# A post-norm decoder layer on one core: the last two down steps interleaved by token tile, transposed x2 in two buffers, side work one step earlier

## What is computed

```python
x = layernorm(x + attention(x))                    # 16 heads, causal, rotary
q, k = ctx @ Wq.T + bq, ctx @ Wk.T + bk            # cross attention, 256 -> 128
x = layernorm(x + einsum('bln,bmn->blm', x, softmax(q @ k.T)))
x = layernorm(x + (silu(x @ w_gate.T) * (x @ w_up.T)) @ w_down.T)   # hidden 2048
```

## Time and profile before

| | us |
|---|---|
| median of three runs | 1038.43 |
| the three runs | 1037.93 to 1039.27 |
| the profiled execution, device time | 1038.01 |
| its span in the trace | 1036.2 |
| TensorE busy | 974.7 |
| mean granted clock of TensorE | 0.99 of full speed |

### The profile page before, as it was taken

The page is one execution under the profiler, slowest core; times in us unless marked ns, Lnnn a source line. Parts: engine busy times, 40 slices in busy tenths (PEclk is TensorE's granted clock), DMA queues, the critical chain, the costliest instruction groups (busy, mean ns, idle before and its releaser), DMA issues.

```text
span 1036.2 us, 15732 instructions
## 1 busy us (share of the span) xinstructions
PE 974.7 (94%) x5416; PEld 789.4 (76%) x5416; DVE 628.6 (61%) x1344; ACT 492.7 (48%) x1075; POOL 352.3 (34%) x353
## 2 busy tenths in 40 slices
PE   7778999999998888999999999999999999999995
PEld 5557777777776666788888788888788888788883
DVE  5687778878775787545544565544665454653443
ACT  5576667767765684244432334432334332333330
POOL 2566646755755442322112132112041111121112
PEclk9999999999999999899999999999999999999998
DMA  5976576755864670262221252221252221243301
GB/s 219 243 190 180 158 182 155 224 146 148 239 159 115 178 209 1 92 237 88 92 92 61 91 208 88 92 92 62 92 218 97 78 86 61 92 173 97 115 2 41
DMA packets 45055, 134.53 MB, mean 130 GB/s; under 512 B 5425, under 2 KB 5553, under 8 KB 42161
## 3 DMA queue, kind: packets, MB, share of 16 engines
q1 hardware_dynamic: 44976, 133.52, 42.5%
HBM read 104.14 MB, written 25.17 MB: 125 GB/s over the span
## 4 chain that ended last, share of the span: by engine, by line
PE 77%; DVE 6%; POOL 5%; issue 5%; ACT 4%; DMA 2%; SPq 0%; POOLq 0%; DVEq 0%; ACTq 0%
PE pg L559 17%; PE pu L559 17%; PE pd L559 17%; PE pj L507 9%; PE pj L559 5%; PE pv L550 4%; PE ps L522 2%; ACT prob L714 2%; PE pa L535 2%; PE pb L535 2%; PE pj L565 1%; DVE prob L911 1%; POOL raw L1139 1%; POOL raw L1144 1%; DMA qk_scratch<-raw 1%
## 5 line engine op out<-in xcount | busy, mean ns | idle before, releaser
L1228 POOL TENSOR_TENSOR g_lo<-gated,g_hi 128x512 fp32r<-128x512 f32 x64 | 82.6, 1290 | 439.5 <-ACT g_hi L805 439.5
L714 ACT ACTIVATE prob<-prob,nmax 128x512 f32<-128x512 f32 (+3 forms) x256 | 143.7, 562 | 106.7 <-DVE nmax L911 106.3
L911 DVE CUSTOM_DVE_ANT_0 prob<-ps,mask 128x512 f32<-128x512 f32 (+3 forms) x256 | 122.9, 485 | 76.9 <-PE ps L522 73.5
L1017 DVE TENSOR_TENSOR dn_lo<-f_raw,dn_hi 128x512 fp32r<-128x512 f32 x64 | 51.3, 802 | 120.9 <-ACT dn_hi L789 120.9
L522 PE MATMUL ps<-ks,qs 128*128 128x256 f32 (+2 forms) x256 | 105.4, 413 | 12.8 <-DVE nmax L911 9.9
L1038 DVE SCALAR_TENSOR_TENSOR half<-th,pg 128x512 f32<-128x512 f32 x64 | 44.0, 688 | 104.3 <-ACT th L796 104.3
L559 PE MATMUL pd<-dn_hi,g_hi 128*128 128x512 f32 x256 | 101.0, 395 | 0.2 <-POOL g_lo L1228 0.2
L796 ACT ACTIVATE th<-pg 128x512 f32<-128x512 f32 x64 | 38.3, 598 | 131.7 <-PE pg L559 131.7
L559 PE MATMUL pd<-dn_lo,g_hi 128*128 128x512 f32 x256 | 99.7, 389 | 0.0
L559 PE MATMUL pd<-dn_hi,g_lo 128*128 128x512 f32 x256 | 99.7, 389 | 0.0
L805 ACT CAST g_hi<-gated 128x512 fp32r<-128x512 f32 x64 | 39.7, 621 | 120.4 <-DVE gated L1045 120.4
(11 more groups left out here) (177 smaller groups left out, 2215.8 us busy)
## 6 DMA issues: line engine op xcount, KB each, us to landing
f_raw<-in_w_ffn SPq DMA_DIRECT2D x64, 768.0 KB, 4.4
qs<-qk_scratch SPq DMA_DIRECT2D x64, 256.0 KB, 4.6
ks<-qk_scratch SPq DMA_DIRECT2D x60, 256.0 KB, 7.7
qk_scratch<-qk_hi SPq DMA_DIRECT2D x32, 256.0 KB, 2.0
qk_scratch<-raw SPq DMA_DIRECT2D x32, 256.0 KB, 2.1
res<-in_x SPq DMA_DIRECT2D x4, 1024.0 KB, 5.0
x_scratch<-res SPq DMA_DIRECT2D x4, 1024.0 KB, 5.2
x<-x_scratch SPq DMA_DIRECT2D x4, 1024.0 KB, 4.8
```

The lines of the kernel that those rows point to most:

```text
L714: act.activation(prob[:, t % PROBS, 0:w], prob[:, t % PROBS, 0:w], ACT.Exp, bias=nmax[:, n % 2, i:i + 1], scale=-1.0, accum_out=rsum[:, n ...
L911: dve.tensor_tensor_reduce(prob[:, t % PROBS, 0:w], ps[:, t % 2, 0:w], mask[:, S - w:S], -D ** -0.5, 3e38, ALU.add, ALU.min, accum_out=nma ...
L1017: dve.tensor_tensor(dn_lo[:, i % 2, :], f_raw[i % NR][:, 2 * KT * P:], dn_hi[:, i % 2, :].bitcast(F32), ALU.subtract).then_inc(dnlo_done, 1)
L1228: pool.tensor_tensor(g_lo[:, i % 2, :], gated[:], g_hi[:, i % 2, :].bitcast(F32), ALU.subtract).then_inc(glo_done, 1)
```

## The change

1. `x2T_hi` and `x2T_lo` get a second buffer; sequence `b` uses number `b % 2`.
2. The side work of `BESIDE` moves one step earlier, and the four `u` transposes are split: tiles 0 and 1 at j = 14, tiles 2 and 3 at j = 15. The load of the context of the sequence after next is issued one place earlier by SyncE, ahead of the store of the output and not behind it.
3. The last step (63) gets banks and buffers of its own: gate and up go to the two banks of `pj`, its halves to `last_hi` and `last_lo`. Its hidden products come before `down(61)`. ScalarE and VectorE split its gate and up weights at the end of step 61 instead of in step 62.
4. The down steps 62 and 63 are interleaved by token tile: three matmuls of step 62 and three of step 63 for tile 0, then tile 1, and so on. Each tile signals `tile_full`, and `finished` waits tile by tile.
5. The last layer norm of tiles 0, 1 and 2 is written by ScalarE, for which GpSimd makes a third small value `nmr2`; tile 3 stays on VectorE. Each tile is stored in a DMA of its own, 256 KB.

```diff
-BESIDE = {3: [("ctx", 0)], 4: [("c", 0)], 5: [("e", 0), ("e", 1)], 6: [("e", 2), ("e", 3)],
+BESIDE = {2: [("ctx", 0)], 3: [("c", 0)], 4: [("e", 0), ("e", 1)], 5: [("e", 2), ("e", 3)],
...
-          11: [("m", 0)], 12: [("m", 1)], 13: [("m", 2)], 14: [("m", 3)], 15: [("u", 0), ("u", 1), ("u", 2), ("u", 3)]}
+          10: [("m", 0)], 11: [("m", 1)], 12: [("m", 2)], 13: [("m", 3)], 14: [("u", 0), ("u", 1)], 15: [("u", 2), ("u", 3)]}
...
+    x2T_hi, x2T_lo = [x2T_hi0, x2T_hi1], [x2T_lo0, x2T_lo1]
...
+    def gate_bank(i):
+        return pj[:, 0, :] if i == STEPS - 1 else pg[:]
+    def up_bank(i):
+        return pj[:, 1, :] if i == STEPS - 1 else pu[:]
+    def gated_halves(i):
+        return (last_hi[:, 0, :], last_lo[:, 0, :]) if i == STEPS - 1 else (g_hi[:, i % 2, :], g_lo[:, i % 2, :])
+    def down_halves(i):
+        return (last_hi[:, 1, :], last_lo[:, 1, :]) if i == STEPS - 1 else (dn_hi[:, i % 2, :], dn_lo[:, i % 2, :])
...
@@ sync
-            if not last:
-                context(b + 1)
+            if b == 0:
+                context(1)
...
             reload(range(HT * b + 2, HT * b + (HT + 2 if not last else HT - NR)))
-            sp.wait_ge(ln_done[1], ST * (b + 1))
-            sp.dma_start(out[b * P:(b + 1) * P, :], fin[:]).then_inc(out_done, 16)
-        sp.wait_ge(out_done, 16 * B)
+            if b < B - 2:
+                context(b + 2)
+            if not last:
+                sp.wait_ge(ln_done[1], ST * (b + 1))
+                sp.dma_start(out[b * P:(b + 1) * P, :], fin[:]).then_inc(out_done, 16)
+        for s in range(ST):
+            if s < ST - 1:
+                sp.wait_ge(tile_done, s + 1)
+            else:
+                sp.wait_ge(ln_done[1], ST * (B - 1) + 1)
+            sp.dma_start(out[(B - 1) * P:B * P, s * E:(s + 1) * E], fin[:, s, :]).then_inc(out_done, 16)
...
@@ tensor
+        def last_down(i, s):
+            if s == 0:
+                pe.wait_ge(dnlo_done, i + 1)
+                pe.wait_ge(glo_done, i + 1)
+            cols = slice(s * P, (s + 1) * P)
+            return three(pd[:, s, :], 1, lambda k: [g[:, cols] for g in gated_halves(i)],
+                         lambda k: down_halves(i), False, i == STEPS - 1)
-        for i in range(1, STEPS):
+        for i in range(1, STEPS - 2):
...
-        down(STEPS - 1)
+        for i in (STEPS - 2, STEPS - 1):
+            hidden(i, 0)
+            hidden(i, 1)
+        down(STEPS - 3)
+        for s in range(ST):
+            last_down(STEPS - 2, s)
+            last_down(STEPS - 1, s).then_inc(tile_full, 1)
...
@@ scalar, at the end
+        for s in range(ST - 1):
+            act.wait_ge(nmr2_done, s + 1)
+            act.activation(fin[:, s, :], fin[:, s, :], ACT.Identity, bias=nmr2[:, s:s + 1],
+                           scale=rstd2[1][:, s, :]).then_inc(tile_done, 1)
...
@@ scalar and vector, in step(i)
-            if i < STEPS - 1:
+            if i < STEPS - 2:
                 gu_half(i + 1)
...
+            if i == STEPS - 3:
+                gu_half(i + 2)
...
@@ vector
+            if b == B - 1:
+                dve.wait_ge(tile_full, s + 1)
+            elif s == 0:
                 dve.wait_ge(d_full, HT * (b + 1))
...
-        for s in range(ST):
-            normalized(B - 1, 1, fin, s)
+        normalized(B - 1, 1, fin, ST - 1)
...
@@ gpsimd, at the end
         for s in range(ST):
             root(B - 1, 1, s)
+            if s < ST - 1:
+                pool.wait_ge(rstd2_done[1], ST * (B - 1) + s + 1)
+                pool.tensor_scalar(nmr2[:, s:s + 1], mv2[1][:, s, 0:1], rstd2[1][:, s, :], -1.0, ALU.mult, ALU.mult).then_inc(nmr2_done, 1)
```

More of the change, by code:

```diff
@@ L161, in program @@
     cqk_hi, cqk_lo = sb("cqk_hi", [P, 2, S], F32R), sb("cqk_lo", [P, 2, S], F32R)
-    x2T_hi, x2T_lo = sb("x2T_hi", [P, KT, S], F32R), sb("x2T_lo", [P, KT, S], F32R)
+    x2T_hi0, x2T_lo0 = sb("x2T_hi0", [P, KT, S], F32R), sb("x2T_lo0", [P, KT, S], F32R)
     f_raw = [sb(f"f_raw{n}", [P, 2 * KT * P + E]) for n in range(2)]
@@ L170, in program @@
     fin = sb("fin", [P, ST, E])
-    sb("unused", [P, 10884 - 1024 + 1024])
+    x2T_hi1, x2T_lo1 = sb("x2T_hi1", [P, KT, S], F32R), sb("x2T_lo1", [P, KT, S], F32R)
+    last_hi, last_lo, nmr2 = sb("last_hi", [P, 2, S], F32R), sb("last_lo", [P, 2, S], F32R), sb("nmr2", [P, ST])
+    sb("unused", [P, 4736])
+    x2T_hi, x2T_lo = [x2T_hi0, x2T_hi1], [x2T_lo0, x2T_lo1]
     flat = pT[:].rearrange("p h n -> p (h n)")
@@ L624, in hidden @@
                     pe.wait_ge(max_done, SCORES)
-                else:
+                elif i < STEPS - 1:
                     pe.wait_ge(gate_read, i)
-            elif i:
+            elif 0 < i < STEPS - 1:
                 pe.wait_ge(gated_done, i)
-            three((pg, pu)[u][:], KT, lambda k: (gu_hi[:, i % 2, u, k, :], gu_lo[:, i % 2, u, k, :]),
-                  lambda k: (x2T_hi[:, k, :], x2T_lo[:, k, :])).then_inc((g_full, u_full)[u], 1)
+            three((gate_bank, up_bank)[u](i), KT, lambda k: (gu_hi[:, i % 2, u, k, :], gu_lo[:, i % 2, u, k, :]),
+                  lambda k: (x2T_hi[i // HT % 2][:, k, :], x2T_lo[i // HT % 2][:, k, :])).then_inc((g_full, u_full)[u], 1)
         def down(i):
@@ L758, in t_half @@
             later, done, hi = {"t": (t1_full, t1hi_done, x1T_hi), "a": (a_full, ahi_done, att_hi),
-                               "u": (t2_full, t2hi_done, x2T_hi)}[kind]
+                               "u": (t2_full, t2hi_done, x2T_hi[b % 2])}[kind]
             filled(act, b, later, kind, n)
@@ L786, in dn_half @@
                 act.wait_ge(av_done, GROUPS)
-            if i >= 2:
+            if 2 <= i < STEPS - 1:
                 act.wait_ge(d_full, i - 1)
-            act.copy(dn_hi[:, i % 2, :], f_raw[i % NR][:, 2 * KT * P:]).then_inc(dnhi_done, 1)
+            act.copy(down_halves(i)[0], f_raw[i % NR][:, 2 * KT * P:]).then_inc(dnhi_done, 1)
         def step(i):
@@ L795, in step @@
                 act.wait_ge(gate_read, i)
-            act.activation(th[:], pg[:], ACT.Tanh, scale=0.5).then_inc(th_done, 1)
-            if i < STEPS - 1:
+            act.activation(th[:], gate_bank(i), ACT.Tanh, scale=0.5).then_inc(th_done, 1)
+            if i < STEPS - 2:
                 gu_half(i + 1)
             if j == HT - 1 and b < B - 1:
-                for s in range(ST):
-                    t_half(b + 1, "u", s)
+                for kind, n in BESIDE[j]:
+                    t_half(b + 1, kind, n)
             act.wait_ge(gated_done, i + 1)
-            if i >= 2:
+            if 2 <= i < STEPS - 1:
                 act.wait_ge(d_full, i - 1)
-            act.copy(g_hi[:, i % 2, :], gated[:]).then_inc(ghi_done, 1)
+            act.copy(gated_halves(i)[0], gated[:]).then_inc(ghi_done, 1)
             if b < B - 1:
@@ L976, in t_half @@
             hi_done, done, hi, lo = {"t": (t1hi_done, t1lo_done, x1T_hi, x1T_lo), "a": (ahi_done, alo_done, att_hi, att_lo),
-                                     "u": (t2hi_done, t2lo_done, x2T_hi, x2T_lo)}[kind]
+                                     "u": (t2hi_done, t2lo_done, x2T_hi[b % 2], x2T_lo[b % 2])}[kind]
             cols = slice(n * P, (n + 1) * P)
@@ L1044, in step @@
                 dve.wait_ge(glo_done, i)
-            dve.scalar_tensor_tensor(gated[:], half[:], 0.5, pu[:], ALU.mult, ALU.mult).then_inc(gated_done, 1)
+            dve.scalar_tensor_tensor(gated[:], half[:], 0.5, up_bank(i), ALU.mult, ALU.mult).then_inc(gated_done, 1)
             steps = BESIDE.get(j, []) if b < B - 1 else []
             if j == HT - 1 and b < B - 1:
-                for s in range(ST):
-                    t_half(b + 1, "u", s)
+                for kind, n in steps:
+                    t_half(b + 1, kind, n)
             beside(b + 1, steps)
@@ L1225, in step @@
             pool.wait_ge(ghi_done, i + 1)
-            if i >= 2:
+            if 2 <= i < STEPS - 1:
                 pool.wait_ge(d_full, i - 1)
-            pool.tensor_tensor(g_lo[:, i % 2, :], gated[:], g_hi[:, i % 2, :].bitcast(F32), ALU.subtract).then_inc(glo_done, 1)
+            hi, lo = gated_halves(i)
+            pool.tensor_tensor(lo, gated[:], hi.bitcast(F32), ALU.subtract).then_inc(glo_done, 1)
             if b < B - 1:
```

20 lines of the change are left out of this document (12 added, 8 removed).

## The result

| | before | changed |
|---|---|---|
| median, us | 1038.85 (4 runs, 1037.93 to 1040.30) | 1028.02 (4 runs, 1026.07 to 1029.37) |
| ratio of the changed kernel's time | | 0.9884, 95% interval 0.9869 to 0.9899 |
| profiled execution, device time | 1038.01 | 1029.37 |
| its span | 1036.2 | 1027.6 |

The changed kernel is 1.2% faster, 10.8 us by the medians; 1027.4 was forecast. Six more runs on another occasion gave 1028.88 us and a ratio of 0.9895 (0.9879 to 0.9911). Spans are given to 0.1 us, and differences that end at a span's end are no better than that.

What follows compares the result with a forecast made beforehand. TensorE, busy 94%, bounds the kernel; gains come only where it stands still or behind its last matmul. Terms 4.20 + 0.46 + 4.09 + 0.42 + 1.90 = 11.07 us off 1038.01 give 1026.9, as median 1027.4; range 1025.8 to 1031.0.

Steps and rivals of the forecast that it cites:

- Term 1: Three sequence ends: splitting the transposes over two steps removes TensorE's wait, 1.40 us each, 4.20 us in all.
- Term 2: Gap ahead of the last down step: down(61) and other matmuls cover the wait for the new halves, 0.46 us gained.
- The margin: Between last hidden product and first product needing the new halves: 3.40 us of matmuls cover 2.85 us, leaving 0.55.
- Term 3: Program end: interleaved down steps let VectorE's 6.20 us block of sums and moments start 4.09 us before TensorE's end.
- Term 4: Last tile's norm: GpSimd's two small operations run fast without VectorE's norms beside them, 0.42 us gained.
- Term 5: Final store: last 256 KB lands in 2.0 us where 1 MB took 3.9, 1.90 us gained.
- Side work: Moved one step earlier at no cost; second sequence's context, the tightest place, lands 2 us before ScalarE asks for it.
- A: Rival at the tail: four stores share one queue, GpSimd's pair stays slow, 1.90 + 0.42 us less gain, 1029.7; chance 0.07.
- B: Rival at the sequence ends: they keep their wait through another late partner, 1031.6 us; chance 0.04.
- C: Rival in sequences 1 and 3: TensorE reads the second x2T buffer slower; 1042.8 us at 20 ns per matmul; chance 0.03.
- D: Rival for the whole kernel: nothing measurable, sequence-end and VectorE gains both failing, 1036 us or more; chance 0.02.

Runs made afterwards that it cites:

- e4: Changed kernel with two x2T buffers, but all four x2 transposes together at j = 15; median 1032.98 us, ratio 0.9938 to the kernel before.
- e1: The changed kernel run again with no edit; median 1028.88 us, ratio 0.9895 to the kernel before.
- e3: Kernel before with only the changed sequence ends: two x2T buffers, side work one step earlier, context load ahead of the store; median 1035.22 us, ratio 0.9959.
- e6: Changed kernel with all four last norms on VectorE, still stored tile by tile; median 1030.51 us, ratio 0.9911 to the kernel before.
- e5: Changed kernel with one 1 MB store for the last sequence; median 1030.17 us, ratio 0.9913 to the kernel before.
- e7: Changed kernel with the last two down steps one after the other, not interleaved; median 1031.73 us, ratio 0.9928 to the kernel before.
- e8: Changed kernel with down(61) ahead of the hidden products of step 63; median 1031.80 us, ratio 0.9923 to the kernel before.
- e2: Changed kernel with the old sequence ends (one x2T buffer, side work in its old steps), so tail only; median 1031.97 us, ratio 0.9931.

## Why the prediction was right, term by term

Times of the changed kernel are those of its first profile.

| term | forecast, us | measured, us | how |
|---|---|---|---|
| 1, sequence ends | 4.20 | 4.05 | 3 x (5.90 + 2.72 - 3.64 - 3.63) |
| 2, gap ahead of the last down step | 0.46 | 0.45 | see below |
| 3, VectorE beside the down steps | 4.09 | 4.08 | last matmul's end to last `mv`: 6.30 before, 2.22 now |
| 4, GpSimd's pair | 0.42 | 0.44 | last `mv` to last norm: 1.41 before, 0.97 now |
| 5, store | 1.90 | 1.62 | last norm's end to the span's end: 4.27 before, 2.65 now |
| sum | 11.07 | 10.64 | |

**Term 1** has the right mechanism, shown by e4. A little is missing since the down step behind transposes took 2.76 to 2.77 us in this profile and 2.73 to 2.74 in the earlier trace rows. In e1's profile it is 2.73, and the two steps last 7.22 us, a gain of exactly the forecast 1.40 for each end. The same 0.03 us stands behind each of the other twelve pairs of transposes, 0.4 us, which makes up for the difference between the sum of 10.64 and the measured 10.2 of the second part. The profiles of e3 and e6 have the 2.77 too, those of e1, e5, e7 and e8 the 2.73 to 2.74, and in e2 and e4 both kinds stand in one execution; with 18 such steps it makes 0.5 us, nearly all of the 0.6 by which the changed kernel's two profiles differ. So it changes from one execution to another, with the same code; its cause stays open.

**Term 2.** From the gate product of step 62 to the end of the last matmul 84 matmuls are done in both kernels. The chain has that product at

```profile
1004.17 2.72 PE pg L559 x12
```

before and now at

```profile
1002.16 2.72 PE pg L588 x12
```

so it took 19.50 us before (to 1023.67) and 19.05 now (to 1021.21), which is 84 x 0.227: nothing stands still any more. The margin was forecast with 0.55 us. GpSimd ended `last_lo` at 1015.78 (1014.50 + 1.28):

```profile
1014.50 1.28 POOL L1284 TENSOR_TENSOR last_lo<-gated,last_hi 128x512 fp32r<-128x512 f32 x1 [4.15 <-ACT last_hi L849]
...
1016.06 0.19 PEld L588 LDWEIGHTS pd<-last_hi 128*128 128x128 f32 x1
1016.28 0.39 PE L588 MATMUL pd<-last_hi 128*128 128x512 f32 x1
```

The weight load of the first matmul behind the wait started at 1016.06 and the matmul at 1016.28. So 0.28 to 0.50 us were left, somewhat less than forecast, but enough. e8 shows what the order is worth when this cover is gone.

**Term 3.** VectorE runs through from 1017.23 to 1023.43, 6.20 us, the same as before; it is the slower of the two, as forecast. The interleaving and the signals by tile share the gain in halves (e7).

**Term 4.** The size was right, and e6 shows the cause. What the prediction said of the third small operation holds too: GpSimd needs 1.22 us a tile (1020.47 to 1021.69). ScalarE's norm of tile 2 ended 0.64 us behind the last `mv`, as it said (0.65).

**Term 5** is the term whose size was most off, by 0.28 us: 2.2 us to landing where the row of equal size gave 2.0. The row was of stores to the scratch, whose destination is one block of 2 KB rows; here the rows lie 8 KB apart in the output. Whether this or something else makes the 0.2 us wasn't tried; the last 0.1 is rounding. The last store took 2.2 in each of the kernels that store by tile with VectorE's pace.

**Side work.** ScalarE asked for the second sequence's context at 453.66, directly behind `g_hi` of step 2, and found it landed, as forecast; no wait for it stands in the trace.

**The rivals.** A needs stores in close order, and e6 has shown that the effect exists, with 0.7 us and not the 1.9 that A gave it, and why it stays away here. B is excluded by the chain at the sequence ends, C by the two `pg` pieces of 2.72 us that read different x2T buffers, and D by the runs.

**The medians.** The sum of the terms (10.6) and the medians' difference (10.8 and, beside e1, 10.5) agree; a single profiled pair (8.6) would have misled by 2 us. The forecast of 1027.4 was 0.6 us too low. Of this 0.4 lies in its starting point, the median of three runs (1038.43), which is 1038.85 with the fourth, and 0.2 in the terms (11.07 against 10.83 by the medians).

## What to carry to other kernels

Where two buffers take turns and tile n + 2 waits for tile n, put other work in between: half of the tiles a step earlier took away 1.4 us each time. It took a second buffer for what the tiles are written to; whether more `pj` banks would have done as well wasn't tried. At the end of a program, let the last accumulations run tile by tile, put work that needs nothing new between the last product and the first use of its result, and count for each engine behind it what it needs per tile; the slowest (here VectorE, 1.52 us against TensorE's 1.36) sets what is left. Store the last tile alone, but not in close order with the others.

## What the runs showed of the hardware

**The same code ahead of the change took between 437.0 and 441.8 us, and most of the difference is granted clock.** The attention part and step 0 aren't touched by any kernel here, so the same ScalarE operation can be looked up in each trace. The 121st starts between 84.7 and 86.2 us. From there to the 151st, 30 operations on, the table of stretches (start and end, length; PE, PEld, DVE, ACT and POOL busy; granted clock; DMA share; GB/s) has for the kernel before, e8, the changed kernel and e6:

```profile
84.78:101.35 16.57, 16.37 (x134) 12.67 (x133) 13.48 (x39) 10.81 (x32) 10.53 (x9) 1.00 0.74 173
```

```profile
86.09:103.96 17.87, 17.60 (x136) 13.64 (x135) 14.08 (x39) 10.95 (x31) 10.34 (x9) 0.94 0.71 162
```

```profile
84.73:103.01 18.28, 18.03 (x137) 13.87 (x135) 14.06 (x39) 10.91 (x31) 10.32 (x9) 0.91 0.69 156
```

```profile
85.02:104.47 19.45, 19.21 (x136) 14.53 (x135) 14.05 (x39) 10.95 (x32) 10.31 (x9) 0.86 0.64 148
```

TensorE is busy nearly all of this stretch, and the lower its clock, the longer it lasts. The five profiles with a clock of 1.00 there (the kernel before, e2, e3, e4, e7) agree to 0.01 us, 16.56 or 16.57; e1 and e5, with 0.91 and 0.92, take 18.35 and 18.26. As e4 and e7 have the changed code and the full clock, the change doesn't make this stretch slower. From the 601st to the 681st operation it is the same: 41.3 us in four of the seven profiles with a clock of 1.00 and 41.6 to 41.8 in the other three (e1, e2, e3), but 42.85 to 42.94 in e4, e6 and e7, with 0.96.

Ahead of the 121st operation the clock doesn't matter as much: the kernel before and the changed one have 0.98 and 0.94 there and reach it at 84.78 and 84.73. TensorE is busy only 64 and 66 of these 84 us. So the 4.75 us by which e6 is later than the kernel before are 0.2 up to the 121st operation, 2.9 and 1.6 in the two stretches, and nothing in the rest. What makes the clock fall in one execution and not in another stays open. For a comparison of traces it means: compare from one operation to another, and look at the granted clock between them.

**Stores in close order.** 256 KB landed 2.2 us after their issue, once 2.3, when issued 0.87 us or more apart, and 2.8 to 2.9 us when issued every half microsecond; 1 MB at once took 3.9. In e6 the DMA engines moved 369 to 381 GB/s without a break while the four stores were under way; by that rate 256 KB take about 0.7 us (an estimate), more than the half microsecond between two issues and less than 0.87.

**VectorE slowed by GpSimd.** In the changed kernel VectorE's split of the last down weights starts while GpSimd's `g_lo` is running:

```profile
1009.06 1.29 POOL L1284 TENSOR_TENSOR g_lo<-gated,g_hi 128x512 fp32r<-128x512 f32 x1 [6.88 <-ACT g_hi L849]
1009.54 1.36 DVE L1071 TENSOR_TENSOR last_lo<-f_raw,last_hi 128x512 fp32r<-128x512 f32 x1 [1.21 <-ACT last_hi L833]
```

The same operation one step earlier, with GpSimd idle, takes 0.69 us (1002.86). It ended at 1010.90, and the next operation of VectorE had its input only at 1010.96, so this cost nothing, but with 0.06 us to spare. The prediction didn't count it.
